# Two-expert blocks: PE addresses the split parts of W1 by a register, and VectorE no longer copies them

## The reference, cut to what matters

```
logits = xf @ gate_w + gate_b
probs = softmax(logits)
top2_vals, top2_idx = top_k(probs, 2)
for each expert e:                       # W1: (8, 128, 256), W2: (8, 256, 128)
    h = gelu(xf @ W1[e] + b1[e])
    y = h @ W2[e] + b2[e]
    out += cw[:, e] * y                  # cw is zero where e is not one of the two
```

## Time and profile before

| | us |
|---|---|
| median of 3 runs | 807.87 |
| the runs | 809.7, 807.87, 807.0 |
| the profiled execution | 811.01 |
| span of its instructions | 809.1 |
| PE busy | 673.3 (83%) |
| VectorE busy | 672.4 (83%) |
| ScalarE busy | 560.1 (69%) |
| GpSimd busy | 555.0 (69%) |

### The profile page before, as it was taken

How to read it: one execution, slowest core, us unless ns; L and a number is a source line. 1 busy time by engine, 2 the same in 40 slices (tenths; PEclk the granted TensorE clock), 3 DMA queues, 4 the chain that set the end, 5 groups by cost and what they waited for, 6 DMA issues and landing times.

```text
span 809.1 us, 20211 instructions
## 1 busy us (share of the span) xinstructions
PE 673.3 (83%) x6427; PEld 385.5 (48%) x6427; DVE 672.4 (83%) x1710; ACT 560.1 (69%) x1092; POOL 555.0 (69%) x572
## 2 busy tenths in 40 slices
PE   4589999999999999999999896471316999999993
PEld 1333334334334344343343345361206998989883
DVE  4689999999899999999999989965626888888872
ACT  4398987897898989989988777520204666656661
POOL 1220586999999999999999998767651555554443
PEclk9689999999999999999999996655556999999997
DMA  8974326236145272262452204111112222222210
GB/s 291 241 163 122 105 104 169 77 129 141 65 154 124 77 195 90 99 165 81 156 121 85 80 30 110 34 42 57 38 44 51 61 64 69 73 69 64 57 35 1
DMA packets 62298, 79.52 MB, mean 98 GB/s; under 512 B 8292, under 2 KB 35009, under 8 KB 62194
## 3 DMA queue, kind: packets, MB, share of 16 engines
q1 hardware_dynamic: 52626, 61.26, 27.9%
q0 software_dynamic: 4960, 8.58, 3.3%
q10 hardware_dynamic: 4608, 8.39, 2.7%
HBM read 57.10 MB, written 22.85 MB: 99 GB/s over the span
## 4 chain that ended last, share of the span: by engine, by line
PE 24%; DVE 24%; issue 19%; POOL 19%; ACT 7%; another core or an unknown queue 3%; DMA 2%; SPq 1%; POOLq 0%; DVEq 0%; ACTq 0%
POOL out_x L668 11%; PE sum_ps L1626 6%; PE score_ps L1612 6%; DVE prob_ring L1051 6%; PE side_ps L1642 6%; DVE w L1051 4%; DVE prob_ring L1062 3%; ACT xn L733 2%; POOL ctx_sb L586 2%; POOL rows_dram L661 2%; POOL ctx_acc L591 2%; ACT w L806 2%; DVE rspread L1073 1%; PE side_ps L1570 1%
## 5 line engine op out<-in xcount | busy, mean ns | idle before, releaser
L668 POOL DMA_INDIRECT out_x<-xn,limit x91 | 91.2, 1003 | 108.1 <-DVE xn L1449 93.0
L1051 DVE SCALAR_TENSOR_TENSOR w<-score_ps,limit 128x1024 f32<-128x1024 f32 x128 | 150.0, 1215 | 13.4 <-PE score_ps L1612 12.9
L1051 DVE SCALAR_TENSOR_TENSOR prob_ring<-score_ps,limit 128x1024 f32<-128x1024 f32 x128 | 149.3, 1208 | 10.1 <-PE score_ps L1612 9.6
L1612 PE MATMUL score_ps<-stack_mem 128*128 128x512 f16 x512 | 140.1, 388 | 16.8 <-DVE prob_ring L1051 10.0
L586 POOL TENSOR_TENSOR ctx_sb<-ctx_sb,rspread 128x512 f32<-128x512 f32 x105 | 135.3, 1288 | 20.5 <-POOL ctx_acc L591 9.3
L806 ACT ACTIVATE prob_ring<-prob_ring 128x1024 f32<-128x1024 f32 x128 | 132.8, 1054 | 20.2 <-DVE prob_ring L1051 20.2
L806 ACT ACTIVATE w<-w 128x1024 f32<-128x1024 f32 x128 | 133.4, 1052 | 8.9 <-DVE w L1051 8.9
L591 POOL TENSOR_TENSOR ctx_acc<-ctx_acc,ctx_sb 128x512 f32<-128x512 f32 x90 | 115.0, 1278 | 7.1
L938 ACT ACTIVATE xn<-score_ps,vec 128x128 f32<-128x128 f32 x364 | 99.9, 385 | 18.3 <-PE score_ps L1572 12.2
L1612 PEld LDWEIGHTS score_ps<-stack_mem 128*128 128x128 f16 x512 | 37.6, 98 | 116.5 <-DVE prob_ring L1051 39.1
L661 POOL DMA_INDIRECT rows_dram<-x,limit x64 | 65.2, 1019 | 27.9 <-issue 18.3
(11 more groups left out here) (247 smaller groups left out, 1585.2 us busy)
## 6 DMA issues: line engine op xcount, KB each, us to landing
rspread<-rinv_dram SPq DMA_DIRECT2D x88, 256.0 KB
stack_mem<-qk_dram SPq DMA_DIRECT2D x56, 256.0 KB, 5.8
ctx_sb<-rows_dram SPq DMA_DIRECT2D x91, 66.5 KB
qk_dram<-qk_hi ACTq DMA_DIRECT2D x16, 256.0 KB, 2.6
qk_dram<-qk_lo ACTq DMA_DIRECT2D x16, 256.0 KB, 6.1
x<-in_adj SPq DMA_DIRECT2D x4, 512.0 KB, 7.4
ctx_sb<-in_adj SPq DMA_DIRECT2D x4, 512.0 KB, 10.2
stack_mem<-qk_dram SPq DMA_DIRECT2D x16, 128.0 KB, 3.6
```

Source lines behind the costliest of these rows:

```text
L668: pool.indirect_dma_start(out_rows, bass.IndirectOffsetOnAxis(target[:, i % AHEAD:i % AHEAD + 1], 0), stage[:, i % AHEAD, :], None, bounds ...
L1051: dve.scalar_tensor_tensor(out=prob_at(s, u), in0=score_ps[:, 2 * u:2 * u + 2, :], scalar=-LIMIT * SCORE, in1=limit[:, k:k + 1, half * HAL ...
L1612: ins = pe.matmul(score_ps[:, h, :], kstack[:, par, h, k * P:k * P + P], qstack[:, par, h, half * HALF:half * HALF + HALF], start=True, st ...
```

## The change

`w1_copy`, its eight slots, VectorE's registers and its register loads are removed, and the semaphore `w1_copied` with them. The parts of W1 lie in another order, (part, half, expert, column), so that the 128 columns that one matmul wants are a slice at `at` of a run of 1024 columns. `hidden` takes four such slices, high and low of each half, at addresses that PE's sequencer computes. PE's register load moves from the end of `second` to the beginning of every fourth block's `hidden`.

```
+        def w1_at(part, k, at):
+            first = (KH * part + k) * E * P
+            return w1_parts[:, first:first + E * P][:, bass.ds(at, P)]
...
-                    if j % 2 == 0:
-                        load_experts(j // 2 + 1)
-                    for i in TWOS[j + 2]:
-                        w1_copy(i, 0)
-                        w1_copy(i, 1)
...
             def hidden(i, e):
                 u = 2 * i + e
                 if e == 0 and i % 2 == 0:
                     pe.wait_ge(blk_lo_ready, i // 2 + 1)
-                pe.wait_ge(w1_copied, u + 1)
+                if u == 0:
+                    pe.wait_ge(w1_split_ready, KH)
+                if e == 0 and i % 4 == 0:
+                    load_experts(i // 4)
+                at = weights_at(i, e)
                 wait(pe, gelu_done, u - 3)
                 for k in range(KH):
-                    hi, lo = [w1_slot(u)[:, (KH * part + k) * P:(KH * part + k + 1) * P] for part in range(2)]
+                    hi, lo = [w1_at(part, k, at) for part in range(2)]
                     ins = three(score_ps[:, u % 4, k * P:k * P + P], hi, lo, blk_hi[:, i % AHEAD, :], blk_lo[:, i % AHEAD, :])
                 ins.then_inc(z_done, 1)
...
                 def next_at():
                     if i + 1 == BLOCKS:
                         return None
-                    if (i + 1) % 4 == 0:
-                        load_experts((i + 1) // 4)
                     return weights_at(i + 1, 0)
```

More of the change, by code:

```diff
@@ L70, in gnn_moe @@
     ROWS = 12
-    COPIES = 8
     TWOS = [range(i, min(i + 2, BLOCKS)) for i in range(0, BLOCKS, 2)]
@@ L145, in gnn_moe @@
         w1_parts = rspread[:, SPREADS // 2:SPREADS, :].rearrange("p r n -> p (r n)").bitcast(F16)
-        w1_split = w1_parts.rearrange("p (e i k n) -> p e i k n", e=E, i=2, k=KH)
+        w1_split = w1_parts.rearrange("p (i k e n) -> p e i k n", e=E, i=2, k=KH)
         ctx_acc = sb("ctx_acc", [P, HALF], F32)
@@ L208, in gnn_moe @@
         stage = xn_flat[:, 2 * T * P:3 * T * P].rearrange("p (r d) -> p r d", r=AHEAD)
-        def w1_slot(u):
-            return (qk_hi, qk_lo)[u % COPIES // 4][:, u % 4, :]
+        def w1_at(part, k, at):
+            first = (KH * part + k) * E * P
+            return w1_parts[:, first:first + E * P][:, bass.ds(at, P)]
         blk_hi, blk_lo = [v[:, :, :].rearrange("p a n -> p (a n)").rearrange("p (r n) -> p r n", r=AHEAD)
@@ L314, in gnn_moe @@
         b2_cleared = sem("b2_cleared")
-        w1_copied = sem("w1_copied")
         b2_step = sem("b2_step")
@@ L1415, in blk_low @@
                                   ALU.subtract).then_inc(blk_lo_ready, 1)
-            experts = [[dve.alloc_register(f"expert_{j}_{n}") for n in range(8)] for j in range(2)]
-            def load_experts(c):
-                last = min(4 * c + 4, BLOCKS)
-                dve.load(experts[c % 2][0:2 * (last - 4 * c)], pe_table[0:1, 8 * c:2 * last])
-            def w1_copy(i, e):
-                u = 2 * i + e
-                at = dve.snap(experts[i // 4 % 2][2 * (i % 4) + e], min_val=0, max_val=(E - 1) * P)
-                wait(dve, z_done, u - COPIES + 1)
-                dve.tensor_copy(w1_slot(u), w1_parts[:, bass.ds(4 * at, 4 * P)]).then_inc(w1_copied, 1)
             def aim(j):
@@ L1538, in _ @@
             dve.wait_ge(w1_split_ready, KH)
-            load_experts(0)
-            for i in range(4):
-                w1_copy(i, 0)
-                w1_copy(i, 1)
             for j in range(3):
@@ L1821, in load_experts, with weights_at @@
                 pe.load(experts[c % 2][0:2 * (last - 4 * c)], pe_table[0:1, 8 * c:2 * last])
+            def weights_at(i, e):
+                return pe.snap(experts[i // 4 % 2][2 * (i % 4) + e], min_val=0, max_val=(E - 1) * P)
             def hidden(i, e):
@@ L1827, in hidden @@
                     pe.wait_ge(blk_lo_ready, i // 2 + 1)
-                pe.wait_ge(w1_copied, u + 1)
+                if u == 0:
[3 more added lines that the diff above has]
+                at = weights_at(i, e)
                 wait(pe, gelu_done, u - 3)
                 for k in range(KH):
-                    hi, lo = [w1_slot(u)[:, (KH * part + k) * P:(KH * part + k + 1) * P] for part in range(2)]
+                    hi, lo = [w1_at(part, k, at) for part in range(2)]
                     ins = three(score_ps[:, u % 4, k * P:k * P + P], hi, lo, blk_hi[:, i % AHEAD, :], blk_lo[:, i % AHEAD, :])
                 ins.then_inc(z_done, 1)
-            def weights_at(i, e):
-                return pe.snap(experts[i // 4 % 2][2 * (i % 4) + e], min_val=0, max_val=(E - 1) * P)
             def second(i, at, next_at):
@@ L1899, in _ @@
             pe.wait_ge(ffn_w_loaded, 16 * (2 * KH + 1))
-            load_experts(0)
-            at = weights_at(0, 0)
             for j in range(2):
@@ L1906, in _ @@
                 hidden(i, 1)
+            at = weights_at(0, 0)
             for i in range(BLOCKS):
```

## The result

| kernel | median us | runs | profiled execution | span |
|---|---|---|---|---|
| before | 807.43 | 4, 805.96 to 809.7 | 811.01 | 809.1 |
| changed | 823.62 | 4, 823.39 to 852.44 | 823.39 | 821.6 |

The ratio is 1.0201, with a 95% interval of 1.0175 to 1.0226: **the change costs 16 us, 2.0%**. (The run of 852.44 is a disturbed one and stands in no comparison.)

What follows compares the result with a forecast made beforehand. It took a VectorE loop to bound the kernel at 3.97 us per pair, then PE's sequencer at 4.18: 42 x (4.18 - 3.97) = 8.8, plus 0.8, less 0.4, gives +9.2 us, forecast 817.0 us, range 803 to 831.

Steps and rivals of the forecast that it cites:

- sixteen computations: PE's sequencer in the changed kernel: four address computations per unit, at 0.12 us each, 1.92 us per pair of blocks.
- four snaps: PE's sequencer in `hidden`: each snap leaves a MOVE of its own, 0.095 us each, 0.38 us per pair.
- two `seconds`: PE's sequencer: four computations and a wait in each `second`, 0.61 us each, 1.22 us per pair.
- turn and half a load: PE's sequencer per pair: the turn's wait, 0.13 us, and half of a register load made once in two pairs, 0.33 us.
- long steps: Some of PE's sequencer steps last longer than the short 0.12 us; they were taken to add 0.2 us per pair.
- The start: Ahead of the first unit, the register load, now behind the low parts, and a snap add 0.8 us.
- The ends: Pairs at either end of the blocks have fewer units, which takes 0.4 us off the sum.
- A: Rival: PE remains the bound, register work hidden by the sequencer's lead; pair 3.5 to 3.6 us, about 792 us; chance 0.12.
- B: Rival: long steps don't follow into the changed kernel; 807 us, no difference that can be told; chance 0.15.
- C: Rival: matmuls with weights at a register cost the sequencer 0.08 us each; pair 4.8 us, 844 us; chance 0.07.
- The loop turn, combination, low parts, copies, normalization, turn: Kernel before: this loop through VectorE, closed at 4.03 us, was taken to set the pair; copies about 1.0 us of it.

Runs made afterwards that it cites:

- e1: Changed kernel, but every unit reads expert 0's parts of W1 at a fixed address, with no snap or address computation in a unit: 799.65 us.
- e2: Changed kernel with the snap moved behind the wait for `gelu_done`, so that snap and first address computation become one instruction: 811.34 us.
- e9: Changed kernel with one more instruction on TensorE's queue per unit, a wait for a semaphore long reached: 839.4 us.
- half-copied kernels: Two kernels: VectorE copies the first expert's parts, PE reads the second's at a register, 807.81 us; the same with the register load moved back to `second`, 805.58 us.
- e12: Kernel before with only GpSimd's indirect DMA of a block's rows replaced by a plain DMA: 789.04 us.
- e14: Kernel before with each block's store as two plain DMAs of 64 rows, one behind the other: 788.63 us.

## Why the prediction was right, and where it wasn't

**The changed kernel's bound** was read rightly: PE's sequencer, with a period of 4.18 forecast and 4.24 measured. The terms, in medians of start-to-start steps: the sixteen computations cost 0.124 to 0.129 us each instead of 0.12, which is 2.02 and not 1.92, because a computation of three operations lasts 46 ns and not 41; the four snaps 0.095 each, as forecast; the two `seconds` 1.21, as forecast; turn and half a load 0.45 against 0.46. That is 4.06 where the forecast had 3.98. The long steps, with the waits that are left, make up the rest, 0.18 against 0.2. So one term, the computations, was mis-sized by 0.1 us per pair; with what the others took off, the pair is 0.06 longer than forecast: 42 x 0.06 = 2.5 us in the sum.

**The start** was forecast at 0.8 and is 1.3 us: the third turn stands at 623.1 against 621.7 us, the first at the same time in both. **The ends** gave back 0.6 and not 0.4. The sum by measured terms, 42 x (4.243 - 3.963) + 1.3 - 0.6 = 12.5, is the difference of the spans.

**The forecast of 817.0** was 6.6 us low. Three of these are the terms above. The rest is that the profiled execution of before, 811.01, was 3.6 us above the median of its runs and the changed kernel's 823.39 was at its median: between the two traces the sum was only 3 us short (820.2 against 823.39), and moving it to the median took another 3 us off. The measured loss of 16 us is well beyond the 9 that were forecast.

**Rivals.** A (PE stays the bound, 792 us) didn't happen. Its 3.5 us for PE's own length was right (3.56), but even the fixed address, without any of the register work, came only to 799.65. B (no long steps, 807) fell: they were there. C (register weights cost 0.08 us each, 844) fell: the matmul that follows without a computation starts after 0.02 us. The sentence from the Trainium skill (Advanced Engine Details and Errata, Sequencer Loop), by which control instructions would be hidden behind queued matmuls, isn't borne out, read as strictly as the prediction reads it, by any of e1, e2 and e9: taking them away shortens a pair, and adding one lengthens it by twice its duration.

**The step that failed** is the first one, what bounds the kernel now. The loop turn, combination, low parts, copies, normalization, turn is what the waits showed, and its links were added up to 3.97 us. But it had no length of its own. With the plain DMA, the same loop with all its work fits into 3.56 us, since some links are as long as the rows say only beside GpSimd's indirect DMA: a normalization of 0.43 us on average instead of 0.34, a combination that starts a median of 1.67 us behind the start of the last matmul that it needs instead of 0.34. Both long numbers were in the trace of before. I read the 0.58 us of idle time ahead of the combination as a wait for PE, whose matmul was long done, and didn't ask what it waited for then. Two things follow that the prediction had wrong in its reasons, though not in its time. The copies by themselves were not what held the kernel: with them behind the normalization it takes as long, and with the plain DMA they fit in at either place. Their removal isn't worth nothing beside the indirect DMA (e1, without copies and without register work, is at 3.81 us a pair against 3.96, 0.8% faster), but it is far from the 0.47 us (3.97 to 3.5) that the prediction names for the case in which nothing else holds PE. And 3.97 is no fixed length to which the sequencer's work is to be compared: PE needs 3.56, and the 0.40 above it go away with the indirect DMA.

**What stays open.** Why an indirect DMA on GpSimd delays TensorE's updates and goes with pauses of PE and SyncE, no run here shows. Nor is it shown why the updates come sooner in the kernels whose sequencer is the bound: their matmuls follow each other less densely, but they also fall at other moments after GpSimd's row. The exchange also put rows at places in block order, and all rows of a block are written (10.33 MB on that queue instead of 8.58), so that where the rows land wasn't told apart from how the DMA is issued. How the 0.40 us splits between late updates, slower VectorE instructions and pauses wasn't separated either. The half-copied kernels weren't run with the plain DMA, so that their misses are put down to the indirect one by inference. Indirect DMAs for two blocks at once, which would halve their number, were not tried.

## What to carry to other kernels

A register address costs PE's sequencer a step of 0.12 us, whatever the matmul behind it, and matmuls of 128x128 in f16 can follow each other at 56 ns: count an engine's own instructions per period, with snaps, waits and computations, before you take an address from a register in a tight group; where a snap must stand, put it directly ahead of the first computation that uses it. When an engine waits for one whose instruction had long ended, the wait is not explained: find what runs meanwhile on the engines that nobody names. And before work is taken out of a loop, put the same work in another place of it: if the time doesn't fall, the loop isn't all that holds the kernel, and the lengths of its links want a second look.

## What the runs showed of the hardware

- With GpSimd's indirect DMA of 128 rows (0.97 to 1.06 us on GpSimd), semaphore updates of TensorE's matmuls come late: a median of 1153 ns after the matmul's start in the kernel before, where 289 is the rule without it. Most late ones arrive in bursts, 0.4 to 0.8 us after GpSimd's row has ended. With a plain DMA of the same rows to fixed places (0.54 us) none is late, nor with two. It costs this kernel 0.40 us per two blocks, 18 us in all. The Trainium skill (Trainium Architecture — The Big Picture, What this means for kernel authors) calls the engines independent processors that don't block one another without a semaphore; the control run doesn't agree, since nothing but GpSimd's store, with the places of its rows, was exchanged and TensorE's updates came 0.86 us sooner.
- PE at times stops for 0.6 to 0.7 us beside an indirect DMA. The kernel before shows three such pauses, the one that has its normalization first ten, the one with the fixed address eight, the changed one none, and with plain DMAs there is none. SyncE's sequencer has steps of 0.6 us or more besides its register loads 11 times from 620 to 790 us in the kernel before and 39 times in the changed one, nearly all of them from 0.0 to 0.1, from 0.7 to 0.85 or at 1.3 us after the start of a DMA_INDIRECT; with plain DMAs there are four at most. The two stop together only in part: three times in the kernel with its normalization first.
- VectorE's normalization of 128x128 (0.34 us alone) takes 0.51 to 0.57 us if it starts 0.4 to 0.6 us after the start of GpSimd's DMA_INDIRECT in the kernel before (37 cases), and up to 0.41 if it starts 0.6 to 0.8 us after it in the kernel that has its normalization first (27 cases); at other moments of these two it takes at most 0.35 us. In the changed kernel none starts in the first of these stretches, and its longest is 0.38. With the plain DMA in the kernel before (e12, e14) the longest is 0.35.
- A wait for a semaphore that is reached already costs PE's sequencer 0.11 us if it is an instruction of its own, and next to nothing if it rides on a computation (51 instead of 46 ns).
- A snap directly ahead of a computation of the same register is fused with it (up to 65 ns in one step); with four of them fused, and a wait of its own back in every second pair, a pair is 0.22 us shorter.
